# 16-head attention on one core: TensorE's and ScalarE's programs written out for 32 units, and new places for the maxima pairs

## The chip, the cores and the metric

One core of a Trainium2 chip runs the whole program. The metric is device microseconds of one execution. TensorE (PE in the rows; PEld is its weight load) multiplies into PSUM, VectorE (DVE) and ScalarE (ACT) read it, GpSimd (POOL) does small vector work, and SyncE (SP) issues transfers.

## What is computed

Two layers of a gated model: cross attention with 16 heads, a routed feed-forward layer, a wide attention and a product-key memory. The change touches the first alone. Per batch b of 8 and head h of 16 (Dh = 16), over 512 queries and 1601 keys:

```python
v = (values @ Wv.T).reshape(N, -1, H, Dh)
k = (keys @ Wk.T).reshape(N, -1, H, Dh)
q = (query @ Wq.T).reshape(N, -1, H, Dh)
energy = jnp.einsum('nqhd,nkhd->nhqk', q, k)
attn = jax.nn.softmax(energy / jnp.sqrt(jnp.float32(EMBED_DIM)), axis=3)
out = jnp.einsum('nhql,nlhd->nqhd', attn, v).reshape(N, -1, H * Dh)
return out @ Wo.T + bo
```

## The kernel before

`attend_heads` (L333) is one block of programs, one for each engine, ordered by semaphores. The work is cut into 32 units: a unit is one batch and a group of 4 heads (B = 8, G = 4, HG = 4). Keys are cut into 13 tiles of 128 (the last has 65), so a unit has NST = 52 score tiles.

Softmax needs the maximum of each row ahead of the exponential, and the scores are computed twice for that. For the unit ahead, `max_product` (L480) multiplies queries as rows with 400 keys, for two heads at a time on the two halves of the array's rows (L490, L492: a pair), into one of two PSUM bank pairs (MBANKS = 2); VectorE reduces each pair to one maximum per head and query (L639). A unit has 32 such jobs. When all are reduced, VectorE makes their negative maxima `nmax` (L643), TensorE turns them (`turn_max`, L495 and L498) into `ps_m`, VectorE splits them into three bf16 parts (L647 to L650, the split), and SP copies the parts into three spare rows of the query operand (`rows_out`, L403), so that the score product itself subtracts the maximum.

For the unit itself `scores` (L500, L506) multiplies a tile of keys with 512 queries into one of three banks, ScalarE takes the exponential (L587) into a ring of eight buffers, and `values` (L509, L514) multiplies it with the widened values; the four heads of a key tile go to four groups of 32 columns, two instructions each, into one PSUM bank. ScalarE copies that bank out when the unit is done (L594), VectorE inverts the sums in three pieces between its reductions (`invert`, L620), GpSimd divides (L695).

The order on TensorE is written by hand in `unit` (L524). A key step kt runs from 1 to 13: four scores of tile kt (in step 13 the first four of the next unit), then the four values of tile kt - 1. The maxima jobs lie between the scores: jobs 10 to 31 of the next unit evenly over the first 38 score tiles, the turn at the end of the scores of step 10, and jobs 0 to 9 of the unit after next one to a tile over the last ten tiles:

```python
todo = min(len(max_jobs), EARLY - (EARLY - len(max_jobs)) * tile // MAX_SPREAD)
...
todo = max(0, EARLY * (tile - EARLY_AT) // (NST - EARLY_AT))
```

TensorE and ScalarE run seven of the eight batches in a hardware loop whose body holds the four units of a batch, and the last batch written out behind it:

```python
with pe.Fori(0, last) as b:
    for g in range(G):
        unit(b, g)
for g in range(G):
    unit(last, g)
```

VectorE's loop (L656) has one unit in its body: 32 reductions with the pieces of `invert` between them, `nmax`, then the wait for the turned maxima and the split. A pair's product waits until the reduction of the pair two before it is done (`m_red`); a score waits for the exponential of the score three before it (`expd`); the first maxima job of a unit also waits for its loads and for the split of the unit before (`m_parts`); the first scores of a unit wait until the parts have landed (`m_in`). SP's loop issues, for each unit, the loads of the unit four ahead (L389 to L397), the three part copies (L408) and four result copies (L415).

Of the kernel before, what the change touches and what calls it, by code (L numbers as in the profile page):

```python
# [30 lines left out]
HG = 4  # L31
# [301 lines left out]
def attend_heads(nc, sem, t):  # L333
# [12 lines left out]
    SCALE = 1.0 / float(D) ** 0.5  # L346
    UNITS = B * G
    NLOAD = 2 * len(Q_PART) + 2 * MAX_PARTS
    INVERT_IN, INVERT_AT = 3, 15
    EARLY, EARLY_AT = 10, 42  # L350
    MAX_SPREAD = 38
    TURN_AT = MAX_SPREAD // HG + 1
    with Stage(nc, "at") as st:
        ks, qs = st.sb("ks", [STACK, SLOTS, HG, KEYS], BF16), st.sb("qs", [STACK, SLOTS, HG, S], BF16)
        kh, qh = st.sb("kh", [P, SLOTS, HG // 2, KEYS], BF16), st.sb("qh", [P, SLOTS, HG // 2, S], BF16)
# [17 lines left out]
        v_wide, v_dense_used, v_ones = sem("at_v_wide"), sem("at_v_dense_used"), sem("at_v_ones")  # L373
        s_mm, expd, pv = sem("at_scores"), sem("at_exp"), sem("at_pv")
        m_mm, m_red, m_all, m_turned, m_parts, m_in = (sem(f"at_max_{n}") for n in ("mm", "red", "all", "turned", "parts", "in"))
        own, acc_out, o_ready, o_stored, ones, inverted = (
            sem(f"at_{n}") for n in ("own", "acc_out", "o_ready", "o_stored", "ones", "inverted"))

        with nc.Block() as block:
# [60 lines left out]
            def _(pe):  # L440
# [39 lines left out]
                def max_product(b, g, u, n):  # L480

                    p, q, c = max_jobs[n]
                    a, w = MSPANS[c]
                    if n == 0:
                        pe.wait_ge(kq_in[g], b * 16 * NLOAD + 16 * NLOAD)

                        pe.wait_ge(m_parts, u + 1)

                    pe.wait_ge(m_red, u * len(max_jobs) + n + 1)
                    nc.tensor.matmul(ps_m[:, n % MBANKS, 0, 0:w], qs[0:MAX_ROWS, g, 2 * p, q * P:q * P + P],  # L490
                                     ks[0:MAX_ROWS, g, 2 * p, a:a + w], start=True, stop=True)
                    nc.tensor.matmul(ps_m[:, n % MBANKS, 1, 0:w], qh[MAX_ROWS:2 * MAX_ROWS, g, p, q * P:q * P + P],  # L492
                                     kh[MAX_ROWS:2 * MAX_ROWS, g, p, a:a + w], start=True, stop=True).then_inc(m_mm, 1)

                def turn_max(u):  # L495

                    pe.wait_ge(m_all, u + 1)
                    nc.tensor.transpose(ps_m[0:HG * QT, 0, 0, 0:P], nmax[:, :], t["ident"][:, :]).then_inc(m_turned, 1)  # L498

                def scores(u, g, n):  # L500
                    kt, j = n // HG, n % HG
# [22 lines left out]
                def unit(b, g):  # L524

                    u = b * G + g
                    nxt, over = ((b, x) if x < G else (b + 1, x - G) if b is not last else None for x in (g + 1, g + 2))
                    done, early = EARLY, 0  # L530
                    for kt in range(1, KT + 1):
                        if kt == KT and nxt is not None:
                            pe.wait_ge(ones, nxt[1] + 1)
                            pe.wait_ge(m_in, u * 48 + 97)
                        for j in range(HG):
                            tile = HG * (kt - 1) + j + 1
                            if kt < KT:
                                scores(u, g, kt * HG + j)
                            elif nxt is not None:
                                scores(u + 1, nxt[1], j)  # L540
                            todo = min(len(max_jobs), EARLY - (EARLY - len(max_jobs)) * tile // MAX_SPREAD)
                            while nxt is not None and done < todo:
                                max_product(nxt[0], nxt[1], u + 1, done)
                                done += 1
                            todo = max(0, EARLY * (tile - EARLY_AT) // (NST - EARLY_AT))
                            while over is not None and early < todo:
                                max_product(over[0], over[1], u + 2, early)
                                early += 1
                        if nxt is not None and kt == TURN_AT:
                            turn_max(u + 1)  # L550
                        if kt == 1:
                            pe.wait_ge(v_wide, u + 1)

                            pe.wait_ge(acc_out, u + 1)
                        for j in range(HG):
                            values(u, g, (kt - 1) * HG + j)

                last = B - 1
                for n in range(len(max_jobs)):
                    key_product(n)  # L560
                    max_product(0, 0, 0, n)
                turn_max(0)
                for n in range(EARLY):
                    max_product(0, 1, 1, n)
                pe.wait_ge(k_out, len(halves))
                first_scores(0, 0)
                with pe.Fori(0, last) as b:
                    for g in range(G):
                        unit(b, g)
                for g in range(G):  # L570
                    unit(last, g)

            @block.scalar
            def _(act):
# [20 lines left out]


                exps(0, 0, range(HG))
                with act.Fori(0, B - 1) as b:
                    for g in range(G):
                        exps(b * G + g, g, range(HG, NST))  # L600
                        exps(b * G + g + 1, (g + 1) % G, range(HG))
                        sums_out(b * G + g)
                for g in range(G):
                    exps((B - 1) * G + g, g, range(HG, NST))
                    if g + 1 < G:
                        exps((B - 1) * G + g + 1, g + 1, range(HG))
                    sums_out((B - 1) * G + g)

            @block.vector
            def _(dve):  # L610
# [22 lines left out]
                def maxima(u, me, behind=None):  # L633

                    for n, (p, q, c) in enumerate(max_jobs):
                        if behind is not None and INVERT_AT <= n < INVERT_AT + 4 * INVERT_IN and (n - INVERT_AT) % 4 == 0:
                            invert(behind, me, (n - INVERT_AT) // 4)
                        dve.wait_ge(m_mm, u * len(max_jobs) + n + 1)
                        nc.vector.tensor_reduce(pmax[:, 2 * p:2 * p + 2, q, c:c + 1], ps_m[:, n % MBANKS, :, 0:MSPANS[c][1]],  # L639
                                                AX.X, ALU.max).then_inc(m_red, 1)  # L640
                    dve.wait_ge(m_red, (u + 1) * len(max_jobs) + MBANKS)

                    nc.vector.tensor_reduce(nmax[:, :], pmax[:, :, :, :].rearrange("p j q c -> p (j q) c"), AX.X, ALU.max, negate=True).then_inc(m_all, 1)  # L643
                    dve.wait_ge(m_turned, u + 1)

                    dve.wait_ge(m_in, u * 48 + 1)
                    me.then(nc.vector.tensor_copy(mpart[:, 0, :], ps_m[0:HG * QT, 0, 0, 0:P]))  # L647
                    me.then(nc.vector.tensor_tensor(mrest[:, 0, :], ps_m[0:HG * QT, 0, 0, 0:P], mpart[:, 0, :], ALU.subtract))
                    me.then(nc.vector.tensor_copy(mpart[:, 1, :], mrest[:, 0, :]))
                    nc.vector.tensor_tensor(mpart[:, 2, :], mrest[:, 0, :], mpart[:, 1, :], ALU.subtract).then_inc(m_parts, 1)  # L650


                OWN_MAX, OWN = 3, 3 + 2
                for u in range(2):
                    maxima(u, Own(dve, own, u, OWN_MAX))
                with dve.Fori(1, UNITS - 1) as u:  # L656
                    me = Own(dve, own, u, OWN)
                    me.n = 2 * OWN_MAX - OWN
                    maxima(u + 1, me, u - 1)
                me = Own(dve, own, UNITS - 1, OWN)  # L660
                me.n = 2 * OWN_MAX - OWN
# [1398 lines left out]
```

## Time and profile before

| | |
|---|---|
| runs | 3745.4 us median of 3 (3743.72 to 3745.9) |
| profiled execution | 3741.73 us, span 3740.1 us |
| mean granted TensorE clock | 0.961 of full speed |
| PE busy over the whole span | 3463.1 us (93%) |
| DVE, ACT busy over the whole span | 2497.5 us (67%), 1561.6 us (42%) |
| 16-head stage | scores of unit 0 start at 316.6 us, the last unit is copied out at 1604.0 us |

Times in the rows are us from the span's start unless they say ns. A row of the timeline merges neighbouring instructions of one kind: start, length of the merged stretch, engine, line, operation, out<-in, shapes, how many, and in brackets how long the engine sat idle before it and what released it. The end of a matmul is modelled, and neighbouring ones overlap, so starts are the safer numbers. "issue" means that the engine waited for nothing that the profile shows.

### The profile page before, as it was taken

The numbers are of one execution on the slowest core, as the hardware profiler recorded it, in microseconds if no ns is written. First come the engines' busy times: TensorE is split into PE (matmuls) and PEld (weight loads), VectorE is DVE, ScalarE is ACT, GpSimd is POOL, SyncE is SP. The second block draws the span as 40 slices with busy tenths as digits, with TensorE's granted clock in tenths as the row PEclk, the third lists the DMA queues.
The fourth block names the chain that finished last, engine by engine and source line by source line (L and its number), as shares of the span: only waits on it lengthen the run. The fifth ranks groups of instructions, "written<-read, shape, count | busy, mean of one in ns | idle before, by whom it ended". The sixth has DMA issues, their size and how long they took to land. (4 is left out here: it accounts for less than half of the span.)

```text
span 3740.1 us, 67012 instructions
## 1 busy us (share of the span) xinstructions
PE 3463.1 (93%) x21900; PEld 2036.9 (54%) x21900; DVE 2497.5 (67%) x5808; ACT 1561.6 (42%) x2718; POOL 227.7 (6%) x251
## 2 busy tenths in 40 slices
PE   8979999999999999966995999996999999999999
PEld 5643222222222222246883444554988989889898
DVE  5538877878787788642002344436888888888885
ACT  4524766767676677721221122212222222222221
POOL 0022000000000000011001000000000000000000
PEclk9977999999999999987997999997999999999999
DMA  6686545544554554051112122113000000000000
GB/s 224 229 246 90 71 62 76 72 60 68 72 70 62 78 69 61 5 175 58 37 37 83 54 68 86 49 58 121 11 11 13 10 11 10 11 13 10 11 10 9
DMA packets 144210, 240.30 MB, mean 64 GB/s; under 512 B 22808, under 2 KB 100224, under 8 KB 143488
## 3 DMA queue, kind: packets, MB, share of 16 engines
q1 hardware_dynamic: 134768, 220.67, 27.6%
q0 software_dynamic: 4608, 12.59, 1.0%
q10 hardware_dynamic: 4624, 4.46, 0.3%
q8 instruction: 105, 1.72, 0.2%
q14 instruction: 105, 0.86, 0.1%
HBM read 170.38 MB, written 66.86 MB: 63 GB/s over the span
## 5 line engine op out<-in xcount | busy, mean ns | idle before, releaser
L639 DVE TENSOR_REDUCE at_pmax<-at_psm 128x2 f32<-128x800 f32 (+1 forms) x1024 | 968.1, 987 | 232.4 <-PE at_psm L492 220.5
L587 ACT ACTIVATE ring<-at_pss 128x512 f32<-128x512 f32 (+1 forms) x1664 | 907.3, 598 | 330.2 <-PE at_pss L506 328.4
L506 PE MATMUL at_pss<-at_qs,at_ks 99*128 99x512 bf16 (+1 forms) x1664 | 583.4, 394 | 26.7 <-issue 19.4
L1648 PE MATMUL mt_psd<-mt_xl,mt_key_in 128*128 128x128 f32 x4096 | 491.2, 279 | 1.8 <-DMA mt_key_out<-m_out 1.8
L1648 PEld LDWEIGHTS mt_psd<-mt_xl,mt_key_in 128*128 128x128 f32 x4096 | 469.8, 193 | 3.2 <-DMA mt_key_out<-m_out 2.0
L514 PE MATMUL at_pso<-ring,at_vw 128*32 128x512 f32 (+1 forms) x3328 | 449.9, 611 | 0.0
L1674 PE MATMUL mt_psu<-mt_key_out,mt_g 128*128 128x256 f32 x2048 | 447.4, 379 | 1.3 <-DVE mt_g L1884 1.3
L506 PEld LDWEIGHTS at_pss<-at_qs,at_ks 99*128 99x128 bf16 (+1 forms) x1664 | 136.1, 98 | 559.9 <-ACT ring L587 408.0
L1674 PEld LDWEIGHTS mt_psu<-mt_key_out,mt_g 128*128 128x128 f32 x2048 | 386.7, 190 | 52.6 <-DVE mt_g L1884 1.4
L490 PE MATMUL at_psm<-at_ks,at_qs 64*128 64x400 bf16 (+1 forms) x1024 | 359.8, 352 | 32.5 <-DVE at_pmax L639 22.0
L492 PE MATMUL at_psm<-at_kh,at_qh 64*128 64x400 bf16 (+1 forms) x1024 | 359.6, 351 | 0.0
L1736 ACT ACTIVATE mt_g<-mt_psd 128x512 f32<-128x512 f32 x256 | 152.9, 598 | 350.8 <-PE mt_psd L1648 350.4
L490 PEld LDWEIGHTS at_psm<-at_ks,at_qs 64*128 64x128 bf16 x1024 | 95.2, 93 | 338.5 <-issue 171.4
L1884 DVE TENSOR_TENSOR mt_g<-mt_psc,mt_g 128x512 f32<-128x512 f32 x256 | 164.0, 682 | 55.5 <-PE mt_psc L1663 55.4
L1235 PE MATMUL aw_pss<-aw_ctxT,aw_gT 128*128 128x512 f32 (+1 forms) x512 | 187.2, 519 | 9.1 <-ACT aw_gT L1330 9.1
L1712 ACT ACTIVATE mt_sims<-mt_psx 128x512 f32<-128x512 f32 x64 | 38.3, 598 | 349.9 <-PE mt_psx L1621 349.9
L1255 PE MATMUL aw_psw<-aw_pT,aw_ctx 128*128 128x512 f32 (+1 forms) x416 | 183.1, 594 | 0.8 <-issue 0.8
L1390 DVE TENSOR_REDUCE aw_peak<-aw_pss 128x1 f32<-128x1601 f32 x32 | 58.4, 1825 | 175.1 <-PE aw_pss L1235 175.1
L1663 PEld LDWEIGHTS mt_psc<-mt_hot_w,mt_hot_m 128*128 128x128 f16 x4096 | 137.1, 98 | 36.3 <-issue 34.9
L1235 PEld LDWEIGHTS aw_pss<-aw_ctxT,aw_gT 128*128 128x128 f32 x512 | 91.1, 193 | 110.2 <-issue 98.5
L1854 DVE TENSOR_TENSOR mt_hot_m<-mt_iota_m,mt_picksT 128x2048 f16<-128x2048 f16 x128 | 150.2, 1213 | 0.0
L1086 ACT ACTIVATE ex_hid<-ex_psh,ex_b 128x256 f32<-128x256 f32 x136 | 62.4, 474 | 209.9 <-PE ex_psh L1051 209.7
(218 smaller groups left out, 3780.4 us busy)
## 6 DMA issues: line engine op xcount, KB each, us to landing
at_ks<-k_dram SPq DMA_DIRECT2D x192, 200.1 KB, 6.6
k_dram<-pj_kp SPq DMA_DIRECT2D x24, 800.5 KB, 5.5
v_dram<-pj_v SPq DMA_DIRECT2D x8, 1664.0 KB, 9.1
at_vd<-v_dram SPq DMA_DIRECT2D x32, 416.0 KB, 10.2
pj_ctx<-ctxT SPq DMA_DIRECT2D x8, 1601.0 KB, 11.7
at_kh<-k_dram SPq DMA_DIRECT2D x128, 100.1 KB, 5.5
aw_ctxT<-ctxT SPq DMA_DIRECT2D x8, 1601.0 KB, 7.1
at_qs<-q_dram SPq DMA_DIRECT2D x192, 64.0 KB, 6.8
```

The source lines that it names most:

```text
L490: nc.tensor.matmul(ps_m[:, n % MBANKS, 0, 0:w], qs[0:MAX_ROWS, g, 2 * p, q * P:q * P + P], ks[0:MAX_ROWS, g, 2 * p, a:a + w], start=True, ...
L492: nc.tensor.matmul(ps_m[:, n % MBANKS, 1, 0:w], qh[MAX_ROWS:2 * MAX_ROWS, g, p, q * P:q * P + P], kh[MAX_ROWS:2 * MAX_ROWS, g, p, a:a + w] ...
L506: nc.tensor.matmul(ps_s[0:r, (NST * g + n) % SBANKS, :], ks[:, g, j, kt * P:kt * P + r], qs[:, g, j, :], start=True, stop=True).then_inc(s ...
L514: nc.tensor.matmul(ps_o[j * 32:(j + 1) * 32, :], vw[0:r, g % 2, kt * HG + j, :], pr[0:r, (NST * g + n) % PRING, :], start=kt == 0, stop=kt ...
L587: nc.scalar.activation(pr[0:r, (NST * g + n) % PRING, :], ps_s[0:r, (NST * g + n) % SBANKS, :], ACT.Exp, scale=SCALE).then_inc(expd, 1)
L639: nc.vector.tensor_reduce(pmax[:, 2 * p:2 * p + 2, q, c:c + 1], ps_m[:, n % MBANKS, :, 0:MSPANS[c][1]], AX.X, ALU.max).then_inc(m_red, 1)
L1235: ins = nc.tensor.matmul(ps_s[:, n, 0:w], gT[:, k, q * P:q * P + P], ctxT[:, s, k, a:a + w], start=k == 0, stop=k == KC - 1)
L1255: ins = nc.tensor.matmul(ps_w[:, m, :], ctx[0:r, kt, m * P:m * P + P], pT[0:r, s, kt, :], start=kt == 0, stop=kt == KT - 1)
L1648: ins = nc.tensor.matmul(ps_d[:, j % 2, y * P:y * P + P], key_in[:, k, j * YB + y, :], xl[:, s, k, :], start=k == 0, stop=k == KC - 1)
L1674: ins = nc.tensor.matmul(ps_u[:, 0:D], g[:, off % 2, y, :], key_out[:, y, :], start=y == 0, stop=y == YH - 1)
L1736: nc.scalar.activation(g[:, off % 2, j * YB:(j + 1) * YB, :], ps_d[:, j % 2, :].rearrange("p (y n) -> p y n", n=P), ACT.Gelu).then_inc(g_o ...
L1884: nc.vector.tensor_tensor(gv, ps_c[:, tb % CRING, h, :].rearrange("p (n u y) -> p y u n", u=2, y=YH), gv, ALU.mult).then_inc(w_out, 1)
```

## The change

1. TensorE's and ScalarE's loops over batches are replaced by straight programs of all 32 units. VectorE, GpSimd and SyncE keep their loops.
2. A plan gives each key step its maxima jobs and their places: steps 1, 4, 6, 8, 11 and 13 have three (ahead of the third score, after the four scores, after the values), the other seven have two (ahead of the fourth score, after the values). Jobs 10 to 31 of the next unit are in steps 1 to 9 and jobs 0 to 9 of the unit after next in steps 10 to 13, as before.
3. The maxima are turned into the second bank pair. Job 0 (first bank pair) no longer waits for the split before it; job 1 does.
4. VectorE makes the reduction of job 0 of the following unit ahead of the split; the three pieces of `invert` stand before jobs 16, 17 and 21 (before: 15, 19 and 23).

```diff
-    INVERT_IN, INVERT_AT = 3, 15
-    EARLY, EARLY_AT = 10, 42
-    MAX_SPREAD = 38
-    TURN_AT = MAX_SPREAD // HG + 1
+    INVERT_IN, INVERT_AT = 3, (16, 17, 21)
+    TURN_AT = 10
+    THREE = (1, 4, 6, 8, 11, 13)
+    NJ = len(max_jobs)
+    EARLY = sum(2 + (kt in THREE) for kt in range(TURN_AT, KT + 1))
+    order = iter([*range(EARLY, NJ), *range(EARLY)])
+    plan = {kt: {place: next(order) for place in ((2, HG, "values") if kt in THREE else (HG - 1, "values"))}
+            for kt in range(1, KT + 1)}
...
+        turned_at = ps_m[0:HG * QT, 1, 0, 0:P]
...
                     if n == 0:
                         pe.wait_ge(kq_in[g], b * 16 * NLOAD + 16 * NLOAD)
+                    if n == 1:
                         pe.wait_ge(m_parts, u + 1)
...
-                    nc.tensor.transpose(ps_m[0:HG * QT, 0, 0, 0:P], nmax[:, :], t["ident"][:, :]).then_inc(m_turned, 1)
+                    nc.tensor.transpose(turned_at, nmax[:, :], t["ident"][:, :]).then_inc(m_turned, 1)
...
+                    def maxima(place, kt):
+                        ahead, v = (nxt, u + 1) if kt < TURN_AT else (over, u + 2)
+                        if place in plan[kt] and ahead is not None:
+                            max_product(ahead[0], ahead[1], v, plan[kt][place])
                     for kt in range(1, KT + 1):
...
                         for j in range(HG):
-                            tile = HG * (kt - 1) + j + 1
+                            maxima(j, kt)
                             if kt < KT:
                                 scores(u, g, kt * HG + j)
                             elif nxt is not None:
                                 scores(u + 1, nxt[1], j)
-                            todo = min(len(max_jobs), EARLY - (EARLY - len(max_jobs)) * tile // MAX_SPREAD)
-                            while nxt is not None and done < todo:
-                                max_product(nxt[0], nxt[1], u + 1, done)
-                                done += 1
-                            todo = max(0, EARLY * (tile - EARLY_AT) // (NST - EARLY_AT))
-                            while over is not None and early < todo:
-                                max_product(over[0], over[1], u + 2, early)
-                                early += 1
+                        maxima(HG, kt)
                         if nxt is not None and kt == TURN_AT:
                             turn_max(u + 1)
...
                         for j in range(HG):
                             values(u, g, (kt - 1) * HG + j)
+                        maxima("values", kt)
...
+                max_product(0, 1, 1, 0)
                 turn_max(0)
-                for n in range(EARLY):
+                for n in range(1, EARLY):
                     max_product(0, 1, 1, n)
...
-                with pe.Fori(0, last) as b:
+                for b in range(B):
                     for g in range(G):
                         unit(b, g)
-                for g in range(G):
-                    unit(last, g)
...
-                with act.Fori(0, B - 1) as b:
-                    for g in range(G):
-                        exps(b * G + g, g, range(HG, NST))
-                        exps(b * G + g + 1, (g + 1) % G, range(HG))
-                        sums_out(b * G + g)
...
+                for u in range(UNITS):
+                    exps(u, u % G, range(HG, NST))
+                    if u + 1 < UNITS:
+                        exps(u + 1, (u + 1) % G, range(HG))
+                    sums_out(u)
...
+                def maxima(u, me, before=None, behind=None):
                     for n, (p, q, c) in enumerate(max_jobs):
+                        if behind is not None and n in INVERT_AT:
+                            invert(behind, me, INVERT_AT.index(n))
+                        if n == 0 and before is not None:
+                            dve.wait_ge(m_all, before + 1)
+                        dve.wait_ge(m_mm, u * NJ + n + 1)
                         nc.vector.tensor_reduce(pmax[:, 2 * p:2 * p + 2, q, c:c + 1], ps_m[:, n % MBANKS, :, 0:MSPANS[c][1]],
                                                 AX.X, ALU.max).then_inc(m_red, 1)
+                        if n == 0 and before is not None:
+                            split(before, me)
...
+                maxima(0, Own(dve, own))
+                maxima(1, Own(dve, own), 0)
                 with dve.Fori(1, UNITS - 1) as u:
                     me = Own(dve, own, u, OWN)
-                    me.n = 2 * OWN_MAX - OWN
-                    maxima(u + 1, me, u - 1)
+                    me.n = OWN_MAX - OWN
+                    maxima(u + 1, me, u, u - 1)
```

`split` holds the wait for the turned maxima and the four instructions that stood at the end of `maxima` before.

## Rows read from the trace of the kernel before

**Rows 1.** Timeline of ScalarE: the copies that end units 0, 3, 4 and 29.

```profile
361.30 0.60 ACT L594 ACTIVATE quad<-at_pso 128x512 f32<-128x512 f32 x1 [1.02 <-PE at_pso L514]
...
479.27 0.60 ACT L594 ACTIVATE quad<-at_pso 128x512 f32<-128x512 f32 x1 [1.02 <-PE at_pso L514]
...
524.47 0.60 ACT L594 ACTIVATE quad<-at_pso 128x512 f32<-128x512 f32 x1 [1.02 <-PE at_pso L514]
...
1537.16 0.60 ACT L594 ACTIVATE quad<-at_pso 128x512 f32<-128x512 f32 x1 [1.02 <-PE at_pso L514]
```

**Rows 2.** Busy time by stretch: length, PE, PEld, DVE, ACT, POOL busy, clock, DMA, GB/s.

```profile
524.50:563.80 39.30, 38.01 (x222) 9.48 (x221) 32.72 (x41) 28.71 (x53) 2.15 (x2) 1.00 0.51 71
```

**Rows 3.** Timeline of TensorE where its program jumps back, after unit 3.

```profile
478.05 1.18 PE L514 MATMUL at_pso<-ring,at_vw 65*32 65x512 f32 x8
482.37 0.61 PE L506 MATMUL at_pss<-at_qs,at_ks 99*128 99x512 bf16 x1 [3.14 <-issue]
```

**Rows 4.** Timeline of TensorE, a key step with two pairs, unit 9.

```profile
710.62 0.39 PE L506 MATMUL at_pss<-at_qs,at_ks 99*128 99x512 bf16 x1
710.94 0.34 PE L490 MATMUL at_psm<-at_ks,at_qs 64*128 64x400 bf16 x1
...
711.22 0.61 PE L506 MATMUL at_pss<-at_qs,at_ks 99*128 99x512 bf16 x2
711.76 0.34 PE L490 MATMUL at_psm<-at_ks,at_qs 64*128 64x400 bf16 x1
...
712.35 1.06 PE L514 MATMUL at_pso<-ring,at_vw 128*32 128x512 f32 x8
713.35 0.39 PE L506 MATMUL at_pss<-at_qs,at_ks 99*128 99x512 bf16 x1
```

**Rows 5.** Timeline of all engines, key step 12 of unit 9, four pairs.

```profile
718.30 1.07 PE L514 MATMUL at_pso<-ring,at_vw 128*32 128x512 f32 x8
...
720.02 3.69 DVE L639 TENSOR_REDUCE at_pmax<-at_psm 128x2 f32<-128x800 f32 x4 [0.42 <-PE at_psm L492]
...
721.97 0.34 PE L490 MATMUL at_psm<-at_ks,at_qs 64*128 64x400 bf16 x1 [0.22 <-DVE at_pmax L639]
...
722.24 1.07 PE L514 MATMUL at_pso<-ring,at_vw 128*32 128x512 f32 x8
```

**Rows 6.** Timeline of TensorE, key step 11 of unit 30, no pairs.

```profile
1565.65 0.82 PE L506 MATMUL at_pss<-at_qs,at_ks 99*128 99x512 bf16 x3
...
1566.79 0.39 PE L506 MATMUL at_pss<-at_qs,at_ks 99*128 99x512 bf16 x1 [0.32 <-ACT ring L587]
```

**Rows 7.** Timeline of all engines around the turned maxima, unit 9.

```profile
714.06 0.99 DVE L639 TENSOR_REDUCE at_pmax<-at_psm 128x2 f32<-128x800 f32 x1 [0.84 <-PE at_psm L492]
...
715.08 0.22 DVE L643 TENSOR_REDUCE at_nmax<-at_pmax 128x16 f32<-128x64 f32 x1
...
715.36 0.28 PE L498 MATMUL at_psm<-ident_sb,at_nmax 128*16 128x128 f32 x1 [0.48 <-DVE at_nmax L643]
...
715.57 1.06 PE L514 MATMUL at_pso<-ring,at_vw 128*32 128x512 f32 x8
715.77 0.28 DVE L647 CAST at_mpart<-at_psm 16x128 bf16<-16x128 f32 x1 [0.47 <-PE at_psm L498]
...
716.64 0.28 DVE L650 TENSOR_TENSOR at_mpart<-at_mrest,at_mpart 16x128 bf16<-16x128 f32 x1
716.95 1.82 SPq L408 DMA_DIRECT2D at_qs<-at_mpart  x3
```

**Rows 8.** VectorE's loop branch (duration ns, starts us), and its next reduction, unit 9.

```profile
L656 DVEq COMPARE_BRANCH  x1: 56/56/56, 716.7 to 716.7; - x1
L656 DVEq FUSED_REGOPS  x1: 74/74/74, 717.0 to 717.0; - x1
...
717.70 1.89 DVE L639 TENSOR_REDUCE at_pmax<-at_psm 128x2 f32<-128x802 f32 x2 [0.78 <-PE at_psm L492]
```

**Rows 9.** Transfers: the split parts into the query operand, KB each, us to landing.

```profile
at_qs<-at_mpart SPq DMA_DIRECT2D x96, 4.0 KB, 1.8
```

More of the change, by code:

```diff
@@ L485, in max_product @@
                         pe.wait_ge(kq_in[g], b * 16 * NLOAD + 16 * NLOAD)
+                    if n == 1:
                         pe.wait_ge(m_parts, u + 1)
-                    pe.wait_ge(m_red, u * len(max_jobs) + n + 1)
+                    pe.wait_ge(m_red, u * NJ + n + 1)
                     nc.tensor.matmul(ps_m[:, n % MBANKS, 0, 0:w], qs[0:MAX_ROWS, g, 2 * p, q * P:q * P + P],
@@ L528, in unit @@
                     u = b * G + g
-                    nxt, over = ((b, x) if x < G else (b + 1, x - G) if b is not last else None for x in (g + 1, g + 2))
-                    done, early = EARLY, 0
+                    nxt, over = ((b, x) if x < G else (b + 1, x - G) if b < last else None for x in (g + 1, g + 2))
+                    def maxima(place, kt):
+                        ahead, v = (nxt, u + 1) if kt < TURN_AT else (over, u + 2)
+                        if place in plan[kt] and ahead is not None:
+                            max_product(ahead[0], ahead[1], v, plan[kt][place])
                     for kt in range(1, KT + 1):
@@ L556, in unit @@
                             values(u, g, (kt - 1) * HG + j)
+                        maxima("values", kt)
                 last = B - 1
-                for n in range(len(max_jobs)):
+                for n in range(NJ):
                     key_product(n)
                     max_product(0, 0, 0, n)
+                max_product(0, 1, 1, 0)
                 turn_max(0)
-                for n in range(EARLY):
+                for n in range(1, EARLY):
                     max_product(0, 1, 1, n)
@@ L597, in _ @@
                 exps(0, 0, range(HG))
-                with act.Fori(0, B - 1) as b:
-                    for g in range(G):
-                        exps(b * G + g, g, range(HG, NST))
-                        exps(b * G + g + 1, (g + 1) % G, range(HG))
-                        sums_out(b * G + g)
[L603 to L607, printed above, removed]
+                for u in range(UNITS):
[3 more added lines that the diff above has]
+                    sums_out(u)
             @block.vector
@@ L631, in invert, with split @@
                         nc.vector.transpose(den[:, :], inv[:, :].unsqueeze(2).broadcast_to([P, S // 32, 32])).then_inc(inverted, 1)
-                def maxima(u, me, behind=None):
-                    for n, (p, q, c) in enumerate(max_jobs):
-                        if behind is not None and INVERT_AT <= n < INVERT_AT + 4 * INVERT_IN and (n - INVERT_AT) % 4 == 0:
-                            invert(behind, me, (n - INVERT_AT) // 4)
-                        dve.wait_ge(m_mm, u * len(max_jobs) + n + 1)
+                def split(u, me):
+                    dve.wait_ge(m_turned, u + 1)
+                    dve.wait_ge(m_in, u * 48 + 1)
+                    me.then(nc.vector.tensor_copy(mpart[:, 0, :], turned_at))
+                    me.then(nc.vector.tensor_tensor(mrest[:, 0, :], turned_at, mpart[:, 0, :], ALU.subtract))
+                    me.then(nc.vector.tensor_copy(mpart[:, 1, :], mrest[:, 0, :]))
+                    nc.vector.tensor_tensor(mpart[:, 2, :], mrest[:, 0, :], mpart[:, 1, :], ALU.subtract).then_inc(m_parts, 1)
@@ L640, in maxima @@
                                                 AX.X, ALU.max).then_inc(m_red, 1)
-                    dve.wait_ge(m_red, (u + 1) * len(max_jobs) + MBANKS)
+                        if n == 0 and before is not None:
+                            split(before, me)
+                    dve.wait_ge(m_red, (u + 1) * NJ + MBANKS)
                     nc.vector.tensor_reduce(nmax[:, :], pmax[:, :, :, :].rearrange("p j q c -> p (j q) c"), AX.X, ALU.max, negate=True).then_inc(m_all, 1)
-                    dve.wait_ge(m_turned, u + 1)
@@ L646, in maxima @@
[L646 to L650, printed above, removed]
                 OWN_MAX, OWN = 3, 3 + 2
-                for u in range(2):
-                    maxima(u, Own(dve, own, u, OWN_MAX))
+                maxima(0, Own(dve, own))
@@ L656, in _ @@
+                maxima(1, Own(dve, own), 0)
                 with dve.Fori(1, UNITS - 1) as u:
                     me = Own(dve, own, u, OWN)
-                    me.n = 2 * OWN_MAX - OWN
-                    maxima(u + 1, me, u - 1)
+                    me.n = OWN_MAX - OWN
+                    maxima(u + 1, me, u, u - 1)
                 me = Own(dve, own, UNITS - 1, OWN)
-                me.n = 2 * OWN_MAX - OWN
+                me.n = OWN_MAX - OWN
+                split(UNITS - 1, me)
                 for u in range(UNITS - 2, UNITS):
```

## The prediction

> **What bounds the kernel now.** I read the completion copies of the units first (the chain of waits ends in a later stage and says nothing of this one), then TensorE's list in order of time, then VectorE's. The change lies in the 16-head stage alone; every stage after it moves as a block, so what is saved here is saved in the whole.
>
> Call S one score product, P one pair of maxima products, V the eight instructions of a value step, T the turned maxima; r is the reduction of a pair, exp ScalarE's work on a score. A unit has 13 key steps of four S and one V, with 32 P spread over them.
>
> The copies that end the units stand 39.32 us apart: unit 0 to unit 3 are 117.97 us for three [rows 1]. Between unit 3 and unit 4 there are 45.20 us, and that is where the TensorE program jumps back. From unit 0 to unit 29 there are 29 gaps and 1175.86 us, which is 35.6 us more than 29 x 39.32 = 1140.3: six jumps at 5.9 us. In one unit TensorE has 38.01 us of work in 39.30, VectorE 32.72, ScalarE 28.71, at a granted clock of 1.00, the 2.4 GHz level [rows 2]. So TensorE sets the pace, but it idles 1.3 us a unit and its matmuls overlap with gaps that a busy share doesn't show. The jump itself: V at 478.05, the next S at 482.37 with 3.14 us idle put down to issue, not to another engine; that S takes 0.61 us [rows 3] against 0.39 elsewhere [rows 4], the lower clock level after the idle stretch. Idle time plus slow products make the 5.9 us.
>
> **Prices inside a step** [rows 4]: a step with two P, from S at 710.62 to S at 713.35, takes 2.73 us: S to P 0.32, P to S 0.28, two S and on to P 0.54, P through the last S to V 0.59, V to S 1.00. Since P to S is 0.27 or 0.28, S to V is 0.32. In a step with four P the reductions rule: they stand (3.69 - 0.99)/3 = 0.90 us apart, and a P may start 0.06 us after the reduction of the pair two before it ends (the second of the four ends at 720.02 + 0.90 + 0.99 = 721.91, P starts at 721.97). From V to V that step takes 722.24 - 718.30 = 3.94 us; P to V is 0.27 [rows 5]. Before, two such steps (12 and 13) end every unit.
>
> A further limit shows where no P is left: three S in 0.82 us, the fourth starts 1.14 us after the first, released by ScalarE, since a score has three banks and needs the exp of the one three before it [rows 6].
>
> **The change, part by part.**
>
> *1. TensorE's and ScalarE's programs written out.* Six back jumps go: -35.6 us [rows 1]. That straight code has no such stall is shown by the same rows: each iteration holds four units in a row at 39.32, and the last four units were outside the loop before. ScalarE's own jump lies in TensorE's gap; it goes with it and is worth nothing of its own. Waits become constants in place of register sums; the straight last units ran no faster, so that is zero. VectorE's, POOL's and SP's loops stay.
>
> *2. Places of the pairs.* Seven steps of a unit now run S S S P S V P, six run S S P S S P V P. The fourth S is reached at 0.21 + 0.21 + 0.32 + 0.28 = 1.02 us after the first, but must wait until 1.14, as in [rows 6]. So two-pair steps cost 1.14 + 0.32 + 1.00 (V to P) + 0.27 = 2.73, exactly the old 2.73: the fewer changes of shape are eaten by the wait for exp. Three-pair steps cost 1.14 + 0.32 + 0.27 + 1.00 + 0.27 = 3.00. P after V stands in no row. I take V to S, 1.00, since it is the same leaving of the four column groups; the low end is 0.89 (less the 0.11 by which S to P exceeds S to S, (0.82 - 0.39)/2 = 0.21), the high end 1.11 (that 0.11 once more).
>
> The reductions keep up: in steps 13 and 1, three P each, P starts 0.53, 1.46 and 2.73 us into the step, r follows 0.39 later (S at 713.35, P 0.32 on, r at 714.06) [rows 4, 7] and six r of 0.90 fit in 6.0 us. The three invert pieces before jobs 16, 17 and 21 shift one reduction by about 0.5 us; the pair two later starts 2 us on, so zero, covered by the bank ring. If it lost that cover, up to 0.5 us a unit.
>
> *3. Step 10, the turned maxima.* Count from V of step 9 = 0. Then P (job 31) 1.00, first S 1.27, its r at 1.39, and the reduction to nmax 1.02 us after r (715.08 - 714.06) [rows 7]: 2.41. T may start 0.28 later, 2.69. Fourth S 2.41, T at 2.73: the old 0.48 us of waiting for nmax [rows 7] vanishes. V at 2.94 (T to V 0.21). The next P may start at 3.94, but it uses the bank in which T lies and now waits for the split. The split is no longer right behind nmax: r of job 0 stands before it. VectorE's branch comes at 716.7 just after its last issue, the next iteration's first register instruction at 717.0 [rows 8]; this 0.3 us was hidden before and now lies between nmax and r, so r starts at about 2.41 + 0.28 + 0.27 = 2.96. Cast 0.90 later at 3.86, and from first cast to the end of the last split 716.64 + 0.28 - 715.77 = 1.15 [rows 7]: 5.01, P at 5.07. **A new stall of 1.13 us a unit**, behind which all S of step 11 queue. For the jump's price the low end is 0; the high end is 0.78, the idle time before r at 717.70 [rows 8], all of which P's own lateness explains. Kept between them: 0.27.
>
> By the Trainium skill (Advanced Engine Details and Errata, Control Flow Timing) compare-and-branch is about 108 ns; the row's own duration is 56 ns but the distance to the next instruction 0.3 us, so the trace decides. By the page's figure this stall would be 0.16 us shorter, 5 us in all.
>
> Behind the split SP issues three transfers (1.82 us [rows 7]) that land 1.8 us after issue [rows 9]: 5.01 + 3.6 = 8.6, while the first S that needs them, in step 13, comes at 5.34 + 3.00 + 2.73 = 11.1. Hidden with 2.5 us over; no transfer is added or moved otherwise. The loads for later units and the value spreading on POOL keep their triggers, which only come 1 us sooner.
>
> *Sum of a unit:* 7 x 2.73 + 6 x 3.00 + 0.21 + 1.13 = 38.45 us, against 39.32: -0.87. It holds for units 0 to 29 (unit 30 has no pairs two ahead, 31 none): -26.1 us. The prologue puts one pair ahead of the turn and one less behind: zero, since ten reductions follow one another there either way.
>
> Total -35.6 - 26.1 = -61.7. The profiled execution took 3741.7 (span 3740.1 and 1.6 around it): 3680.0. The median of the runs is 3.7 above it: **3684 us**.
>
> **The rivals.**
>
> *A, TensorE alone decides (chance 0.13).* If exp doesn't hold the fourth S, the steps cost 2.61 and 2.88, 0.12 x 13 x 30 = 47 us less: 3637. A V to P of 0.89 gives nearly the same (43 us): 3641. For it: each step has one change of shape fewer. Against: the printed wait in [rows 6]. The Trainium skill (TensorEngine Tiling (Array Packing), Key Properties) says that a change of tiling mode drains TensorE; the 0.11 us of S to P over S to S agrees. It gives no size; counted at that 0.11 for the one change fewer in each step, and with no wait for exp, the rule would give 43 us less, 3641.
>
> *B, the pairs bring nothing (0.12).* The split chain is longer (the jump at 0.78, the cast kept from following r at 0.90): stall 1.9 to 2.0 and the gain of 0.87 is gone: 3710. The change would then not do what it says for the pairs.
>
> *C, straight code stalls too (0.06).* If the long program waits for its instructions here and there, half the 35.6 is lost: 3702. Against: the straight stretches in [rows 1].
>
> *D, slower (0.04).* V to P is dear: the pair needs both halves of the rows, and V's four column groups end one by one. It decides from 61.7/(30 x 13) = 0.16 us over V to S; at 0.25 over it, so 1.25 us, it costs 0.25 x 30 x 13 = 97 us and the time is 3684 + 97 = 3781. Against: leaving V for S costs 1.00, and P into V costs no more than P into S.
>
> The forecast itself has 0.65. Its own bounds: the jump -8 to +15, V to P -43 to +43, the rounding of 13 steps +-4. I don't add the ends: 3655 to 3714 holds the forecast, B and C, and leaves out A and D and the tails, under 2 in 10. A measurement of this kernel can tell about 0.2%, 7.5 us, from no change. Faster 0.94, the same 0.02, slower 0.04.
>
> **What would show it.** Right: copies of the units at 38.4 to 38.5 us everywhere, no 3 us issue gap; the four fourth scores still waiting for exp; V to P near 1.00; one idle stretch of about 1.1 us a unit before the second early pair, released by the last split; queued reductions still 0.90 apart. Wrong: a pitch under 37.5 (A), over 39 (B), gaps put down to issue (C), V to P over 1.1 (D), or a wait of the first S of step 13 for the transfers.

## The result, and the profile after

The changed kernel takes 3687.3 us (median, 3683.7 to 3691.0) against 3744.6 us of the kernel before in the same session: ratio 0.9848, 95% interval 0.9831 to 0.9865, faster by 57 us. The forecast was 3684 us. The profiled execution took 3685.97 us with a span of 3684.2 us. One of the four executions of experiment 2 took 5674 us at a mean granted clock of 0.552 and isn't counted in its median.

Line numbers have moved: scores are L512 now, pairs L496 and L498, the turn L504, values L520, exponentials L591, reductions L650, nmax L656, the split L637 to L640.

The timeline of ScalarE in the changed kernel, copies at the ends of units 0 to 3 and of unit 29:

```profile
361.25 0.60 ACT L598 ACTIVATE quad<-at_pso 128x512 f32<-128x512 f32 x1 [0.40 <-PE at_pso L520]
...
399.88 0.60 ACT L598 ACTIVATE quad<-at_pso 128x512 f32<-128x512 f32 x1 [0.39 <-PE at_pso L520]
...
438.77 0.60 ACT L598 ACTIVATE quad<-at_pso 128x512 f32<-128x512 f32 x1 [0.39 <-PE at_pso L520]
...
477.38 0.60 ACT L598 ACTIVATE quad<-at_pso 128x512 f32<-128x512 f32 x1 [0.39 <-PE at_pso L520]
...
1482.43 0.60 ACT L598 ACTIVATE quad<-at_pso 128x512 f32<-128x512 f32 x1 [0.39 <-PE at_pso L520]
```

Against [rows 1]: unit 0 to unit 3 is 116.13 us (117.97 before), and there is no 45 us gap anywhere. From unit 0 to unit 29 there are 1121.18 us, 54.7 less than the 1175.86 before. 23 of the 29 units take 38.6 us; six, like the one that ends at 438.77, take 38.9. The rest of the program gives another 1.2 us, within what two executions differ by (the four of the changed kernel lie 7 us apart).

Busy time by stretch, columns as in [rows 2]:

```profile
524.50:563.00 38.50, 37.05 (x223) 9.25 (x221) 33.05 (x41) 27.38 (x53) 2.14 (x2) 1.00 0.56 72
```

The same work now fills 38.5 us, not 39.3: VectorE was busy 32.72 of 39.30 and is busy 33.05 of 38.50.

TensorE's timeline, a key step with two pairs (unit 9):

```profile
672.46 1.06 PE L520 MATMUL at_pso<-ring,at_vw 128*32 128x512 f32 x8
673.46 0.34 PE L496 MATMUL at_psm<-at_ks,at_qs 64*128 64x401 bf16 x1
...
673.73 0.82 PE L512 MATMUL at_pss<-at_qs,at_ks 99*128 99x512 bf16 x3
674.49 0.34 PE L496 MATMUL at_psm<-at_ks,at_qs 64*128 64x400 bf16 x1
...
674.87 0.39 PE L512 MATMUL at_pss<-at_qs,at_ks 99*128 99x512 bf16 x1
675.19 1.06 PE L520 MATMUL at_pso<-ring,at_vw 128*32 128x512 f32 x8
676.19 0.34 PE L496 MATMUL at_psm<-at_ks,at_qs 64*128 64x400 bf16 x1
```

V to V is 2.73 us, exactly as in [rows 4]. P now follows V after 1.00 us, the number that no row of before showed. The three S stand 0.21 apart and P 0.76 after the first; the fourth S starts 1.14 us after the first although P left TensorE free 0.11 us sooner (P to S is 0.27, here 0.38): it waits for the exponential, as in [rows 6]. The list of all engines has the exponentials of this step and the weight load that belongs to the fourth S:

```profile
674.22 2.06 ACT L591 ACTIVATE ring<-at_pss 128x512 f32<-128x512 f32 x4 [0.94 <-PE at_pss L512]
...
674.87 0.10 PEld L512 LDWEIGHTS at_pss<-at_qs,at_ks 99*128 99x128 bf16 x1 [0.29 <-ACT ring L591]
```

One exponential takes 0.60 us (mean of L591), so the first ends at 674.82 and the load follows at 674.87, released by ScalarE.

All engines around the turn, unit 8 of the changed kernel (V of step 9 is the first row):

```profile
656.55 1.07 PE L520 MATMUL at_pso<-ring,at_vw 128*32 128x512 f32 x8
...
657.55 0.34 PE L496 MATMUL at_psm<-at_ks,at_qs 64*128 64x400 bf16 x1
...
658.97 0.22 DVE L656 TENSOR_REDUCE at_nmax<-at_pmax 128x16 f32<-128x64 f32 x1
...
659.24 0.28 PE L504 MATMUL at_psm<-ident_sb,at_nmax 128*16 128x128 f32 x1
...
659.45 1.06 PE L520 MATMUL at_pso<-ring,at_vw 128*32 128x512 f32 x8
659.56 1.00 DVE L650 TENSOR_REDUCE at_pmax<-at_psm 128x2 f32<-128x802 f32 x1 [0.38 <-DVE at_nmax L656]
660.47 0.27 DVE L637 CAST at_mpart<-at_psm 16x128 bf16<-16x128 f32 x1
...
661.34 0.28 DVE L640 TENSOR_TENSOR at_mpart<-at_mrest,at_mpart 16x128 bf16<-16x128 f32 x1
...
661.67 0.34 PE L496 MATMUL at_psm<-at_ks,at_qs 64*128 64x400 bf16 x1 [1.16 <-DVE at_mpart L640]
```

Against [rows 7]: T no longer idles for nmax, and a stretch of 1.16 us of idle time before job 1 has taken its place, released by the last split instruction.

### The profile page after: what moved, and what is told of

Read it like the earlier page. It is cut to its first block and busy times, and to the rows that moved or that the text cites. A ratio compares the mean times of both kernels' runs of the same rounds, so it can differ in the third digit from the quotient of the medians.

```text
span 3684.2 us, 63095 instructions
## 1 busy us (share of the span) xinstructions
PE 3419.8 (93%) x21900; PEld 2028.1 (55%) x21900; DVE 2509.6 (68%) x5808; ACT 1513.7 (41%) x2718; POOL 227.2 (6%) x251
## 3 DMA queue, kind: packets, MB, share of 16 engines
q8 instruction: 86, 1.41, 0.2%
## 5 line engine op out<-in xcount | busy, mean ns | idle before, releaser
L650 DVE TENSOR_REDUCE at_pmax<-at_psm 128x2 f32<-128x800 f32 (+1 forms) x1024 | 980.3, 989 | 181.1 <-PE at_psm L498 151.5
L591 ACT ACTIVATE ring<-at_pss 128x512 f32<-128x512 f32 (+1 forms) x1664 | 858.6, 602 | 341.2 <-PE at_pss L512 341.2
L512 PE MATMUL at_pss<-at_qs,at_ks 99*128 99x512 bf16 (+1 forms) x1664 | 527.1, 388 | 16.6 <-ACT ring L591 8.1
L520 PE MATMUL at_pso<-ring,at_vw 128*32 128x512 f32 (+1 forms) x3328 | 444.1, 606 | 0.0
L496 PEld LDWEIGHTS at_psm<-at_ks,at_qs 64*128 64x128 bf16 x1024 | 95.0, 93 | 602.5 <-DVE at_pmax L650 327.1
L496 PE MATMUL at_psm<-at_ks,at_qs 64*128 64x400 bf16 (+1 forms) x1024 | 356.2, 348 | 46.5 <-DVE at_mpart L640 36.3
L498 PE MATMUL at_psm<-at_kh,at_qh 64*128 64x400 bf16 (+1 forms) x1024 | 356.0, 348 | 0.0
L512 PEld LDWEIGHTS at_pss<-at_qs,at_ks 99*128 99x128 bf16 (+1 forms) x1664 | 129.9, 98 | 267.1 <-ACT ring L591 161.6
L1891 DVE TENSOR_TENSOR mt_g<-mt_psc,mt_g 128x512 f32<-128x512 f32 x256 | 164.0, 683 | 55.8 <-PE mt_psc L1670 55.7
L1719 ACT ACTIVATE mt_sims<-mt_psx 128x512 f32<-128x512 f32 x64 | 38.2, 597 | 350.1 <-PE mt_psx L1628 350.1
L1359 ACT ACTIVATE aw_prob<-aw_pss,aw_shift 128x1601 f32<-128x1601 f32 x32 | 51.1, 1597 | 237.5 <-DVE aw_shift L1400 237.1
```

Source lines behind the costliest of these rows:

```text
L512: nc.tensor.matmul(ps_s[0:r, (NST * g + n) % SBANKS, :], ks[:, g, j, kt * P:kt * P + r], qs[:, g, j, :], start=True, stop=True).then_inc(s ...
L1891: nc.vector.tensor_tensor(gv, ps_c[:, tb % CRING, h, :].rearrange("p (n u y) -> p y u n", u=2, y=YH), gv, ALU.mult).then_inc(w_out, 1)
```

## The experiments

Times are medians; each ratio is to the kernel before on the same chip, with its 95% interval.

**1. Programs written out, pairs in their old places.**

```diff
-                with pe.Fori(0, last) as b:
+                for b in range(B):
                     for g in range(G):
                         unit(b, g)
-                for g in range(G):
-                    unit(last, g)
```

and the same for ScalarE, in the kernel before.

> The kernel before with TensorE's and ScalarE's programs written out, the pairs in their old places. My theory (the two parts add, the jump is 35.6 us): units 39.32 us apart throughout, no idle stretch put down to issue, 3709 us (3705 to 3713). Rival (straight code stalls as well, or the back jumps cost less than the gaps in the old timeline say): gaps at other places and over 3720 us.

Measured 3707.5 us, ratio 0.9895 (0.9879 to 0.9912), 38.2 us less than the 3745.7 of the kernel before. ScalarE's timeline, the copies at the place where the jump was:

```profile
479.94 0.60 ACT L592 ACTIVATE quad<-at_pso 128x512 f32<-128x512 f32 x1 [1.02 <-PE at_pso L514]
...
519.24 0.60 ACT L592 ACTIVATE quad<-at_pso 128x512 f32<-128x512 f32 x1 [1.02 <-PE at_pso L514]
```

The gap of 45.20 us is 39.30 now, and units 0 to 29 span 1140.0 us, against 1140.3 worked out in the prediction. Straight code has no such gap: my theory held, and the rival fell.

**2. Places only, both loops kept.** The changed kernel with the loops of before.

> The changed kernel with both loops put back, so only the places of the pairs and the order of the split are new. My theory: units 38.60 us apart inside an iteration, the six gaps of about 5.9 us still there, 3744.6 - 29 x 0.72 = 3724 us (3719 to 3728). Rival (the pairs bring nothing, the whole gain is the jump): 3745.

Measured 3723.8 us (median of three, 3722.8 to 3732.0), 0.9939 (0.9919 to 0.9959): 22 us less, 3724 us expected. The rival fell. The profiled execution is the slowest of the three. In it most units inside an iteration take 38.68 us, 0.08 more than in the changed kernel; the second unit of each iteration takes 39.0; four units took 40.1 to 40.4 us (6 us in all); and the six gaps cost 31.2 us, where the kernel before has 35.6. Experiments 4 and 8 show what the four long units are. The two parts of the change, 38 and 22 us, add up to 60 where both together gave 57: they are separate to within some 3 us, about what the executions of one kernel differ by.

**3. TensorE's loop alone back.**

> The changed kernel with TensorE's loop back and ScalarE's program written out. My theory: ScalarE's jump lay inside TensorE's gap, so this equals the run with both loops, 3724 us within 4. Rival (the two jumps follow one another, or ScalarE's late jump prolongs TensorE's): 5 to 20 us below the run with both loops.

Measured 3724.3 us, 0.9941 (0.9924 to 0.9957). That is the time with both loops (3723.8). The six gaps cost 30.3 us, 0.9 less than with both loops: the jumps lie side by side. My theory held.

**4. ScalarE's loop alone back.**

> The changed kernel with ScalarE's loop back and TensorE's program written out. If ScalarE's jump costs about what TensorE's did (3.1 us idle and a lower clock after it), it is exposed now, since the next exp is due 0.5 us after its copy: six gaps of 3 to 6 us, 3705 to 3723 us. Rival (ScalarE's jump is short, its code stays at hand): no gap, 3687 us, and the 0.27 us by which an exp comes late in every fourth unit of the changed kernel is gone or moved.

Measured 3725.5 us, 0.9942 (0.9924 to 0.9959), 2.5 us over the upper end of what I expected. Gaps of 42.5 to 45.3 us, 32.6 us in all over the pitch: ScalarE's jump alone costs about as much as both. ScalarE's waits in this kernel (us in total, times, longest):

```profile
ACT ring L591 <- issue: 16.1, 6, 2.8
```

So ScalarE's half of the first edit, "worth nothing of its own" in the prediction, is worth nothing while TensorE jumps and 38 us once TensorE doesn't, the long units below included. Of two engines that stop at the same time each hides the other.

Two other units of this kernel took 40.1 us, and in two of the units that begin with a jump step 12 takes the same 1.5 us more, so that the jumps themselves cost some 29.6 of the 32.6 us, 4.9 each. Busy time by stretch in one of them, columns as in [rows 2]:

```profile
737.00:746.00 9.00, 8.92 (x54) 2.26 (x53) 7.78 (x10) 6.44 (x14) 0.52 (x1) 1.00 0.44 72
746.00:755.00 9.00, 7.80 (x44) 1.66 (x43) 6.80 (x11) 5.39 (x11) 0.00 (x0) 0.91 0.03 8
755.00:764.00 9.00, 9.00 (x52) 2.33 (x52) 6.84 (x8) 6.34 (x13) 0.88 (x1) 0.90 0.17 39
```

(the last three numbers are the granted clock, DMA's share and GB/s), and TensorE's timeline there:

```profile
751.29 0.34 PE L496 MATMUL at_psm<-at_ks,at_qs 64*128 64x400 bf16 x1 [1.16 <-DVE at_mpart L645]
...
753.30 1.88 PE L520 MATMUL at_pso<-ring,at_vw 128*32 128x512 f32 x8
755.12 0.51 PE L496 MATMUL at_psm<-at_ks,at_qs 64*128 64x401 bf16 x1
```

Behind the idle 1.16 us of step 10 the mean granted clock of the two stretches is 0.91 and 0.90; V takes 1.88 us for 1.06 and P 0.51 for 0.34, the lower level (1.2 GHz) in place of 2.4. The changed kernel has the same idle stretch and no such unit.

**5. The split directly behind nmax.** To show that the new idle stretch is what stands ahead of the split:

```diff
                         if n == 0 and before is not None:
                             dve.wait_ge(m_all, before + 1)
+                            split(before, me)
...
                                                 AX.X, ALU.max).then_inc(m_red, 1)
-                        if n == 0 and before is not None:
-                            split(before, me)
```

> The changed kernel with VectorE's split put back directly behind the negative maxima, ahead of the reduction of job 0. My theory (the 1.16 us idle stretch of step 10 is the reduction and the branch that stand ahead of the split): first cast about 0.41 us behind the turn, the idle stretch before job 1 falls from 1.16 to about 0.4 us, two short waits of 0.1 to 0.2 us for reductions come up in step 11, units about 38.1 us apart, 3673 us (3669 to 3679). Rival (the reduction of job 0, late now, holds the pairs of step 11 as long as the split did): 3687.

Measured 3667.1 us, 0.9797 (0.9781 to 0.9814); units 37.92 us apart. All engines around the turn:

```profile
654.94 0.28 PE L504 MATMUL at_psm<-ident_sb,at_nmax 128*16 128x128 f32 x1
...
655.42 0.28 DVE L637 CAST at_mpart<-at_psm 16x128 bf16<-16x128 f32 x1 [0.54 <-PE at_psm L504]
...
656.63 0.34 PE L496 MATMUL at_psm<-at_ks,at_qs 64*128 64x400 bf16 x1 [0.42 <-DVE at_mpart L640]
```

The cast comes 0.48 us behind T (1.23 in the changed kernel) and the idle stretch is 0.42 us. The units are 0.68 us shorter, where I had expected 0.5, and the time is 2 us under the lower end of what I expected: the pairs of step 11 hardly wait for the late reduction. The rival fell.

**6. Job 1 later.** Step 10 keeps one pair, job 1 goes ahead of the third score of step 11, step 12 gets three.

```diff
-    THREE = (1, 4, 6, 8, 11, 13)
+    THREE, ONE = (1, 4, 6, 8, 11, 12, 13), 10
...
-    plan = {kt: {place: next(order) for place in ((2, HG, "values") if kt in THREE else (HG - 1, "values"))}
+    plan = {kt: {place: next(order) for place in ((2, HG, "values") if kt in THREE else (HG - 1,) if kt == ONE else (HG - 1, "values"))}
```

> The changed kernel with job 1 moved from behind the values of step 10 to ahead of the third score of step 11 (step 10 has one pair, step 12 three). My theory: TensorE does 0.5 us of scores first, the idle stretch falls from 1.16 to about 0.6 us, units 38.0 to 38.1 us apart, 3670 us (3666 to 3677). Rival (VectorE is the bound in steps 11 to 13 with nine pairs in 9 us): 3687 or more.

Measured 3668.3 us, 0.9807 (0.9790 to 0.9823); units 37.95 us apart, and TensorE's idle time before job 1:

```profile
620.65 0.34 PE L496 MATMUL at_psm<-at_ks,at_qs 64*128 64x400 bf16 x1 [0.62 <-DVE at_mpart L640]
```

0.62 us, as expected. Nine pairs in steps 11 to 13 are not too many for VectorE.

**7. Both edits.**

> Both edits: the split directly behind the negative maxima, and job 1 ahead of the third score of step 11. My theory: the split is done before job 1 comes up, no idle stretch, 7 steps of 3.01, 5 of 2.74, one of 2.46 and 0.21 for the turn: units 37.45 us apart, 1.15 less than in the changed kernel, 3653 us (3648 to 3660). Rival (as before, VectorE becomes the bound): over 3670.

Measured 3647.1 us, 0.9746 (0.9730 to 0.9762), some 38 us faster than the changed kernel by the ratios, 40 by the medians; units 37.38 us apart, 37.45 expected, and the time is 1 us under the lower end of what I expected. In the changed kernel TensorE's waits for other engines between 400 and 1450 us are these two rows (us in total, times, longest):

```profile
PE at_psm L496 <- DVE at_mpart L640: 31.3, 27, 1.2
PE at_pss L512 <- ACT ring L591: 1.6, 6, 0.3
```

and with both edits only this one is left:

```profile
PE at_pss L512 <- ACT ring L591: 1.6, 6, 0.3
```

**8. Both edits, with TensorE's and ScalarE's loops back.**

> The kernel of both edits with TensorE's and ScalarE's loops back. Some units of the kernels with a loop took 1.5 us more, with TensorE at the lower clock level right after the 1.2 us idle stretch of step 10. My theory (that idle stretch sets the dip off): with no idle stretch the six gaps at the jumps stay, about 5.2 us each, and no unit inside an iteration takes over 37.8 us; 3647 + 31 = 3678 us (3672 to 3684). Rival (the dips come with the loops whatever TensorE does in step 10): two to five units 1.5 us longer.

Measured 3678.9 us, 0.9837 (0.9821 to 0.9853). The six gaps cost 31.1 us and no other unit is longer than 37.66. With loops and the idle stretch, TensorE fell to the lower clock in step 12 of two to four units (four in experiments 2 and 4, two in 3); with loops and no idle stretch, of none. One execution stands behind each of these counts. So in these executions the dips came only with the idle stretch. Why the changed kernel, which has the stretch and no loops, shows none isn't settled.

**9. VectorE written out in the changed kernel.**

```diff
-                with dve.Fori(1, UNITS - 1) as u:
+                for u in range(1, UNITS - 1):
```

> The changed kernel with VectorE's program written out too. My theory: the reduction of job 0 follows the negative maxima by 0.25 us instead of 0.59, so the idle stretch shrinks by 0.34 us, units 38.26 us apart, 3677 us (3673 to 3682). Rival (the 0.59 is the wait for the negative maxima, not the branch): 3687.

Measured 3678.2 us, 0.9825 (0.9809 to 0.9842); units 38.26 us apart, as worked out. VectorE and TensorE at the turn:

```profile
618.05 0.22 DVE L656 TENSOR_REDUCE at_nmax<-at_pmax 128x16 f32<-128x64 f32 x1
618.30 0.99 DVE L650 TENSOR_REDUCE at_pmax<-at_psm 128x2 f32<-128x802 f32 x1
...
618.32 0.28 PE L504 MATMUL at_psm<-ident_sb,at_nmax 128*16 128x128 f32 x1
...
620.41 0.34 PE L496 MATMUL at_psm<-at_ks,at_qs 64*128 64x400 bf16 x1 [0.82 <-DVE at_mpart L640]
```

r follows nmax by 0.25 us instead of 0.59: VectorE's jump is worth 0.34 us here and the idle stretch is 0.82 us. The rival fell.

**10. The same with both edits in.**

> The kernel of both edits (split directly behind the negative maxima, job 1 ahead of the third score of step 11) with VectorE's program written out as well. My theory: the branch lies under the turn and the split now waits for the turn alone, so the 0.34 us that writing out gave to the changed kernel are worth nothing here: units 37.38 us apart, 3647 us (3643 to 3651). Rival (every engine's loop costs on its own): another 10 us less, 3637.

Measured 3646.8 us, 0.9749 (0.9733 to 0.9765), units 37.37 us apart: nothing more to gain. With the split first, the jump lies under the turn.

**11. Values ahead of the fourth score.** An attempt to get rid of the wait for the exponential, on top of both edits:

```diff
-                        for j in range(HG):
-                            maxima(j, kt)
...
-                        maxima(HG, kt)
+                        for j in range(HG - 1):
+                            score(j)
+                        maxima(HG - 1, kt)
...
                         maxima("values", kt)
+                        score(HG - 1)
+                        maxima("end", kt)
```

> The kernel of both edits with the values of a step moved ahead of its fourth score (two pairs: S S S P V S P; three: S S S P V P S P), and ScalarE's copy ahead of its last exp of the next unit. My theory (each step loses 0.12 us because the fourth score waits for the exp of the first): two-pair steps 2.61 us, three-pair steps 2.88, step 10 about 2.8 with 0.4 us of waiting for the negative maxima, units 36.0 us apart, and units 30 and 31 shorter too: 3601 us (3594 to 3612). Rival (VectorE with 32.7 us of work in 36 becomes the bound, the pairs wait for reductions): units over 36.8 us apart, over 3625.

The kernel that ran leaves ScalarE's copy where it was, other than the expectation says; step 1, whose V waits for that copy, takes 3.01 us as in experiment 7, so this cost nothing.

Measured 3668.0 us, 0.9808 (0.9791 to 0.9824): some 21 us slower than without it, units 37.98 us apart, every fourth 38.5 to 38.8. Neither reading held. The time is one that the rival gave, but TensorE never idles for a reduction here. From V to V the steps take 2.73 and 3.01 us, as before, one more of them than before takes 3.01, and step 10 grew from 2.89 to 3.22, with 0.2 us of idle time before T. Together that is the 0.60 us a unit. TensorE's timeline, one step:

```profile
569.46 1.06 PE L520 MATMUL at_pso<-ring,at_vw 128*32 128x512 f32 x8
570.46 0.39 PE L512 MATMUL at_pss<-at_qs,at_ks 99*128 99x512 bf16 x1
570.78 0.34 PE L496 MATMUL at_psm<-at_ks,at_qs 64*128 64x400 bf16 x1
...
571.05 0.93 PE L512 MATMUL at_pss<-at_qs,at_ks 99*128 99x512 bf16 x3
571.92 0.34 PE L496 MATMUL at_psm<-at_ks,at_qs 64*128 64x400 bf16 x1
...
572.19 1.06 PE L520 MATMUL at_pso<-ring,at_vw 128*32 128x512 f32 x8
```

The hold has moved to the third of the next three scores: 571.05 + 0.93 - 0.39 = 571.59, 1.13 us after the score at 570.46. With three banks any score waits for the exponential of the one three before it, so the rule counts over every four scores in a row, not over the first four of a step. My sum had applied it to one place only. A step has one gap between scores that holds V; the other three must fill 1.14 us, and with one pair among them they fill 1.02. Put both pairs there and they fill 1.41, but then V stands alone in its gap at 1.32, and the step is 2.73 once more. By this count a fourth score bank would lift it; that wasn't tried. In every fourth unit 0.5 us more stands in step 13: the first score of a batch goes to the same bank as the last of the batch before (`scores` counts banks within a batch), and here the two stand close together.

## Why the prediction was right

*The jumps (-35.6 us).* Right. Experiment 1 gave 38 us in the medians and 35.8 in the units of the profile (1175.86 to 1140.03), and no wait of the changed kernel's TensorE in the stage is put down to issue (rival C). That ScalarE's jump is "worth nothing of its own" was too strong, as experiment 4 shows: true of what is removed first, wrong of what is removed last. It didn't touch the sum, since the change removes both.

*The places of the pairs (0 in steps 1 to 9).* Right: 2.73 and 3.01 us against 2.73 and 3.00. V to P, bounded by 0.89 and 1.11, is 1.00. The fourth score waits at 1.14 us as it did where no pairs were left. Rival A needed that wait not to bind, and it binds; experiment 11 met it again in another place. Rival D needed V to P at 1.16 or more.

*The new stall (1.13 us).* Right in kind, place and size: 1.16 us. T comes 2.69 us after V of step 9 (I had 2.73), nmax to r takes 0.59 (0.55), r to the first cast 0.91 (0.90), first cast to the end of the last 1.15 (1.15). Experiments 5, 6, 7 and 9 each take a part of it away, and the units shrink by 0.68, 0.65, 1.22 and 0.34 us, where the idle stretch shrinks by 0.74, 0.54, 1.16 and 0.34. Rival B needed a stall of 1.9 us or more. The price of the branch, 0.27 in the forecast, is 0.34: that much nearer to nmax r comes when VectorE's loop is taken away (experiment 9). By the Trainium skill (Advanced Engine Details and Errata, Control Flow Timing) compare-and-branch takes about 108 ns; the whole of the jump costs more here.

*The transfers behind the split.* Hidden, as forecast; no wait of a score for them is in the list of waits.

*The sum.* 38.60 us a unit for 38.45 (0.15 x 29 = 4.4 us), and six units with 0.27 us more (1.6 us), which I had not seen: the forecast's sign of 38.4 to 38.5 us everywhere did not come true. These 6 us are the difference between the 61.7 us forecast and the 55.8 us by which the profiled executions differ. Most of the 0.15 is in step 11: from V of step 10 to V of step 11 it takes 4.24 us, where 3.00 and the stall of 1.13 were counted. Some of the closeness is luck: the forecast set the median 3.7 us above the profiled execution, as in the kernel before, and in the changed kernel it lies 1.3 above, which brought 2.4 of the 6 us back.

## What to carry to other kernels

Read the waits between neighbouring instructions as a small table of prices and count with it per step; busy shares of 97% before and 96% after would have told nothing of either part of this change. Where an edit makes a wait later on one engine, walk through what now stands ahead of the instruction that releases it: here a reduction of 0.9 us and a loop's branch of 0.3 made a wait that took back 1.2 of the 1.9 us a unit that the places could give (39.30 to 37.38), and putting the split ahead of that reduction returned 20 us. Where several engines' loops jump at the same place, take them all away or none: here one alone gave nothing.

## What the runs showed of the hardware

A jump back over four units' code leaves TensorE idle for 3.0 to 3.5 us in the kernel before and 2.8 to 3.5 in experiment 3; with the lower clock behind it, 5.9 us are lost a jump in the kernel before and 5.1 in experiment 3. The same jump leaves ScalarE idle for 2.4 to 2.8 us, with some 4.9 us lost by the whole (experiment 4). VectorE's jump over one unit's code costs 0.34 us. Why a jump costs 5.9 us with the old places and 5.2 with the new (experiments 2 and 8) isn't shown. The Trainium skill (Runtime: NRT & Kernel Launch, Instruction fetch mechanics) says that a taken branch whose target is outside the part of the program at hand has to wait for a fetch, and that straight code is fetched ahead. The trace agrees: the changed kernel's page has (queue, kind: packets, MB, share of 16 engines)

```profile
q8 instruction: 86, 1.41, 0.2%
q14 instruction: 81, 0.66, 0.1%
```

and both counts are 105 in the kernel before, whose program is shorter; with one loop back, one of the two goes back to 105 (q8 in experiment 3, q14 in experiment 4). Code that is jumped back over is fetched again.

The 0.27 us in every fourth unit come from ScalarE. ScalarE's and TensorE's timeline in the unit of the changed kernel that took 38.89 us:

```profile
402.95 0.82 PE L512 MATMUL at_pss<-at_qs,at_ks 99*128 99x512 bf16 x3
...
403.71 2.06 ACT L591 ACTIVATE ring<-at_pss 128x512 f32<-128x512 f32 x4 [1.22 <-PE at_pss L512]
...
404.37 0.39 PE L512 MATMUL at_pss<-at_qs,at_ks 99*128 99x512 bf16 x1 [0.32 <-ACT ring L591]
```

The first exponential starts 0.76 us after its score instead of 0.49, with nothing else late, and the fourth score waits 0.27 us longer. It isn't a price of straight code. The same late exponential is in the trace of every kernel here, with a loop or without, about once in four units: at the same six places of the program in each kernel whose ScalarE program is written out, and at one place of the loop's body, in its second unit, in each that has the loop. The kernel before has it too (all engines, unit 5):

```profile
538.54 0.39 PE L506 MATMUL at_pss<-at_qs,at_ks 99*128 99x512 bf16 x1
...
539.31 2.06 ACT L587 ACTIVATE ring<-at_pss 128x512 f32<-128x512 f32 x4 [0.96 <-PE at_pss L506]
...
539.97 0.39 PE L506 MATMUL at_pss<-at_qs,at_ks 99*128 99x512 bf16 x1
```

There two pairs stand between the first and the fourth score, which are 1.43 us apart anyway, and the 0.77 us of the exponential are hidden. The new places, with 1.02 us between them, bring it out: experiment 2, places only, has units of 39.0 us, and experiment 1, straight code only, has one of 39.6 in place of 39.3 among 29. Since it goes with the place in the program, it may be the fetch of code; no run tested that.
